# The skip term of a state space layer: a diagonal product on TensorE, or a multiply-add on VectorE

## The reference

```python
x_conv = silu(causal_conv(x_ssm) + conv_b)         # 4 taps
B_mat, C_mat = split(x_conv @ W_x + b_x)           # 16 states each
A_discrete = exp(-exp(A_log))
h = A_discrete * h + xc_t[:, :, None] * B_t[:, None, :]
y = einsum('bn,bdn->bd', C_t, h) + D_param * xc_t  # the skip term is D_param * xc_t
y = y * silu(gate)
y = y @ W_out + b_out
```

## Time and profile before

| | |
|---|---|
| median of 3 runs | 522.19 us |
| profiled execution | 522.04 us |
| its span on the core | 520.2 us |
| TensorE (PE) busy | 440.5 us, 85% |
| VectorE (DVE) busy | 395.1 us, 76% |
| GpSimd (POOL) busy | 386.6 us, 74% |
| ScalarE (ACT) busy | 290.6 us, 56% |
| chain that ended last, by engine | PE 60%, DVE 15%, ACT 10%, issue 9% |

### The profile page before, as it was taken

The page is one execution under the profiler, slowest core; times in us unless marked ns, Lnnn a source line. Parts: engine busy times, 40 slices in busy tenths (PEclk is TensorE's granted clock), DMA queues, the critical chain, the costliest instruction groups (busy, mean ns, idle before and its releaser), DMA issues.

```text
span 520.2 us, 6106 instructions
## 1 busy us (share of the span) xinstructions
PE 440.5 (85%) x1807; PEld 263.3 (51%) x1807; DVE 395.1 (76%) x683; ACT 290.6 (56%) x475; POOL 386.6 (74%) x317
## 2 busy tenths in 40 slices
PE   0784968899799989998999899989999899786653
PEld 0563844665367446754665457545655476332221
DVE  2174042885899799779997999789997979779985
ACT  2664463875467745775477647763866466433300
POOL 2554342877878988988799889977998888755583
PEclk9988797989999999999999999999999999898966
DMA  8400001721162216221633144222423152225220
GB/s 305 168 20 4 2 1 34 189 81 42 41 167 61 84 34 202 82 81 42 174 98 94 40 130 137 80 60 74 149 82 81 53 151 81 82 72 151 72 91 20
DMA packets 25379, 46.97 MB, mean 90 GB/s; under 512 B 3072, under 2 KB 4096, under 8 KB 25088
## 3 DMA queue, kind: packets, MB, share of 16 engines
q1 hardware_dynamic: 24336, 45.13, 30.2%
q10 hardware_dynamic: 1008, 1.41, 0.8%
HBM read 42.33 MB, written 4.19 MB: 89 GB/s over the span
## 4 chain that ended last, share of the span: by engine, by line
PE 60%; DVE 15%; ACT 10%; issue 9%; POOL 3%; DMA 2%; SPq 0%; DVEq 0%; ACTq 0%; POOLq 0%
PE bank0a L941 28%; PE bank1a L1021 6%; DVE hs L1371 6%; PE bank0a L1060 5%; DVE xbank L1348 4%; PE ybank L1086 3%; PE bank1a L1031 3%; PE bank1a L1006 3%; ACT xn L694 2%; PE bank0d L914 2%; DMA Bt<-w_in 1%; DVE st L1276 1%; PE ybank L1081 1%; PE bank0d L930 1%; PE bank1d L1054 1%
## 5 line engine op out<-in xcount | busy, mean ns | idle before, releaser
L556 POOL TENSOR_TENSOR hs<-hs,Ct 128x512 f32<-128x512 f32 x127 | 165.1, 1302 | 39.3 <-DVE hs L1371 24.1
L1371 DVE TENSOR_TENSOR_SCAN hs<-decay,carry,xbank 128x512 f32<-128x512 f32 x63 | 80.6, 1279 | 7.9 <-DVE xbank L1348 0.5
L1371 DVE TENSOR_TENSOR_SCAN hs<-decay,xbank 128x512 f32<-128x512 f32 x64 | 78.0, 1219 | 5.2
L518 POOL TENSOR_TENSOR hidAl<-plain,hidAh 128x512 fp32r<-128x512 f32 x48 | 66.3, 1384 | 19.2 <-ACT hidAh L653 11.9
L518 POOL TENSOR_TENSOR hidBl<-plain,hidBh 128x512 fp32r<-128x512 f32 x48 | 66.9, 1397 | 16.2 <-ACT hidBh L653 8.2
L1348 DVE TENSOR_TENSOR xbank<-xs,bbank 128x512 f32<-128x512 f32 x104 | 71.6, 689 | 7.0 <-ACT bbank L750 5.3
L652 ACT ACTIVATE plain<-bank0a,col 128x512 f32<-128x512 f32 x64 | 44.0, 687 | 39.1 <-PE bank0a L941 36.1
L941 PE MATMUL bank0a<-hidAh,hTh 128*128 128x512 f32 x128 | 55.9, 437 | 1.7 <-ACT q L685 1.7
L941 PE MATMUL bank0a<-hidBh,hTh 128*128 128x512 f32 x128 | 55.9, 437 | 1.7 <-ACT q L685 1.7
L941 PE MATMUL bank0a<-hidAl,hTh 128*128 128x512 f32 x128 | 51.9, 406 | 0.0
L941 PE MATMUL bank0a<-hidBl,hTh 128*128 128x512 f32 x128 | 51.1, 399 | 0.0
(11 more groups left out here) (190 smaller groups left out, 923.9 us busy)
## 6 DMA issues: line engine op xcount, KB each, us to landing
xs<-x_rows SPq DMA_DIRECT2D x128, 256.0 KB, 3.4
xt<-x_tok SPq DMA_DIRECT2D x8, 256.0 KB, 4.8
xr<-x_feat SPq DMA_DIRECT2D x8, 256.0 KB, 8.2
x_rows<-xc SPq DMA_DIRECT2D x8, 256.0 KB, 2.1
out<-xr SPq DMA_DIRECT2D x7, 256.0 KB, 5.4
fh<-h_w SPq DMA_DIRECT2D x1, 1024.0 KB, 9.8
hs<-h_w SPq DMA_DIRECT2D x1, 1024.0 KB, 11.6
lw<-l_w ACTq DMA_DIRECT2D x1, 640.0 KB, 5.6
```

What stands on the lines that cost most here:

```text
L518: pool.tensor_tensor(low[:, m, :], plain[:, k % NPLAIN, :], high[:, m, :].bitcast(F32), ALU.subtract).then_inc(hidden_low, 1)
L556: pool.tensor_tensor(h, h, Ct[:, hs_(u)], ALU.mult).then_inc(p_ready, 1)
L1371: dve.tensor_tensor_scan(hs[:, i % NSTATES, :], decay[:, gr:gr + 1].broadcast_to([P, HALF]), xbank[:], 0.0 if u % 2 == 0 else carry[:, k:k ...
```

## The change

The diagonal product and `d_diag` go. The first gathering product of each quarter now opens the sum (`start=(quad == 0)`). VectorE adds the skip term when it gates: one `scalar_tensor_tensor` writes xc * D + `ybank` to `yg`, a wait for its own result follows (`y_summed`), and a `tensor_tensor` multiplies `yg` by `gate` in place. In `finish_last` both sums come first, and then both products.

```diff
-            act.activation(d_diag[:], ident[:], ACT.Copy, scale=scale("D")).then_inc(d_ready, 1)
...
-                    if quad == 0:
-                        pe.wait_ge(d_ready, 1)
-                        pe.matmul(ybank[:], d_diag[:], xc[:, hs_(u)], start=True, stop=False)
...
-                                  start=False, stop=(quad == NGRP // QUAD - 1)).then_inc(y_full, 1)
+                                  start=(quad == 0), stop=(quad == NGRP // QUAD - 1)).then_inc(y_full, 1)
...
-                dve.tensor_tensor(yg[:, hs_(t)], ybank[:], gate[:, hs_(t)], ALU.mult).then_inc(yg_ready, 1)
+                dve.scalar_tensor_tensor(yg[:, hs_(t)], xc[:, hs_(t)], scale("D"), ybank[:], ALU.mult,
+                                         ALU.add).then_inc(y_summed, 1)
+                dve.wait_ge(y_summed, t + 1)
+                dve.tensor_tensor(yg[:, hs_(t)], yg[:, hs_(t)], gate[:, hs_(t)], ALU.mult).then_inc(yg_ready, 1)
...
                 for part in range(2):
-                    dve.tensor_tensor(yg[:, quarter(part)], ybank[:, half_of(part)], gate[:, quarter(part)],
+                    dve.scalar_tensor_tensor(yg[:, quarter(part)], xc[:, quarter(part)], scale("D"), ybank[:, half_of(part)],
+                                             ALU.mult, ALU.add).then_inc(y_summed, 1)
+                for part in range(2):
+                    dve.wait_ge(y_summed, t + 1 + part)
+                    dve.tensor_tensor(yg[:, quarter(part)], yg[:, quarter(part)], gate[:, quarter(part)],
                                       ALU.mult).then_inc(yg_ready, 1)
```

More of the change, by code:

```diff
@@ L209, in program @@
         b_conv = sb("b_conv", [P, 1])
-        d_diag = sb("d_diag", [P, P])
         gat = sb("gat", [P, 2 * P // QUAD - DPG])
@@ L363, in program @@
         y_full = sem("y_full")
-        d_ready = sem("d_ready")
+        y_summed = sem("y_summed")
         yg_ready = sem("yg_ready")
```

## The result

The changed kernel takes 514.47 us (median of 4 runs, 513.99 to 515.65), the kernel before 521.92 us beside it. The ratio is 0.9864, 95% interval 0.9833 to 0.9895. Two more comparisons gave 0.984 (0.979 to 0.9889) and 0.9867 (0.9838 to 0.9896). So it is faster, as forecast, but by 7.0 to 7.7 us and not by 4.6.

What follows compares the result with a forecast made beforehand. TensorE was taken to bound seven of eight units: 522.04 - 6.02 + 0 + 0.7 + 0.77 = 517.5 us, so 517.6 expected in the runs. Range 516.6 to 518.8, or 516.2 to 520.8 with the thin cover.

Steps and rivals of the forecast that it cites:

- TensorE bounds seven of eight units and the join moves by 0.86 us each time: Periods 0 to 6: losing the diagonal product brings each join on VectorE 0.86 us earlier, 6.02 us in all.
- the unmoved join: Rival: SiLU behind its table load, or GpSimd's last low part, holds the join; 523.7 us, slower; chance 0.09.
- VectorE's additions are covered: Slot 11, six joins: the longer `gate_y` fits in VectorE's idle time ahead of the join and costs nothing.
- the first kind of period: Three joins with 2.23 to about 2.5 us idle before, none in slots 11 to 15: price about 0.7 us.
- the second kind: Three joins with 2.62 us idle before and a wait in slot 12: price 1.7 us, cover at least 1.93.
- The thin cover: Rival: VectorE and GpSimd block each other whole instructions, each `gate_y` costs 1.9 us; 520.0 us; chance 0.21.
- its fourth case, VectorE as the bound: Rival: over 2.7 us for each `gate_y` before all gain is lost; at 2.7, about 522 to 523; chance 0.04.
- Period 7, +0.7: Last period, where the chain runs on VectorE through `gate_y`: 0.7 us more, between 0.7 and 1.9, all on the path.
- The end, +0.77: `finish_last`: two multiply-adds go first, so the first product starts 0.77 us later, between 0.6 and 1.0, all serial.
- the start-up at nothing: Start-up: ScalarE's making of `d_diag` is one small instruction beside TensorE's first hidden layer, so its removal gains nothing.

Runs made afterwards that it cites:

- e1: The kernel before without the diagonal product and `d_diag`, VectorE unchanged, so the skip term is missing: 513.02 us, ratio 0.9769.
- p1: The changed kernel with the `value` product in slot 14 of TensorE done twice in each of 8 periods: 524.12 us, ratio 1.0054.
- e3: The changed kernel with the diagonal product back only in the loop copy that is not run, and `d_diag` made again: 517.36 us, ratio 0.9848.
- h1: The changed kernel with the diagonal product kept on TensorE for the last unit alone, whose end is as before: 514.43 us.
- l1: The changed kernel with the diagonal product back for units 0 to 3, only in the copy not run, and `d_diag` made: 518.03 us, ratio 0.994.
- both remedies: The changed kernel with the needed loop copy placed first and the last unit's diagonal product kept on TensorE: 512.48 us, ratio 0.9835.
- e4: The kernel before with the diagonal product left out only of the loop copy that is not run: 520.24 us, ratio 0.992.
- e2: The changed kernel with the diagonal product and `d_diag` put back, so the skip term is added twice: 524.68 us, ratio 0.9978.
- e5: The changed kernel with one more product of two SBUF tensors in `gate_y` of units 0 to 5: 513.79 us, ratio 0.9833.

## Why the prediction was wrong

- **TensorE bounds seven of eight units and the join moves by 0.86 us each time:** right. 6.22 us in place of 6.02. It is TensorE's time alone (e1), and another product of that size, `value`, does the same (p1). SiLU moved along, the third GELU still waiting 0.72 us for TensorE as forecast, so the unmoved join did not occur.
- **VectorE's additions are covered:** right. The idle time ahead of the joins stayed above zero. The price in the first kind of period was 1.21 to 1.26 us, by the idle time that is missing against e1, and not 0.7, so only 0.4 us of cover were left. At the place itself it was 0.65, but the compare in slot 12 then met GpSimd (1.85 us at 267.92). It isn't fixed either: at the first of these joins four profiles with the same VectorE work in slot 11 (e3, h1, l1 and both remedies) kept 1.35 us of idle time and not 0.40. In the second kind it was 1.64 at the place (3.86 us from the sum at 314.03 to the next `times_b`, before 2.22), near the 1.7, and 1.28 to 1.39 by the idle time, so up to 1.73 us were left and not 1.4 at most. The thin cover did not decide anything. The prediction's sum for its fourth case, VectorE as the bound, is off as well: with the waits in slot 12 counted, the mean cover plus 0.86 us is about 3.0 us, not 2.7.
- **Period 7, +0.7:** right: from the sum at 470.53 to the next `times_b` at 473.09 are 2.56 us, before 1.91, so +0.65.
- **The end, +0.77:** right at 0.78, measured to the start of the projection. The other 0.52 us of that execution were the clock.
- **The step that failed** is the one that cost the start-up at nothing: "ScalarE's making of `d_diag` is one small instruction in the start-up [...]: nothing", and that the opening by four products "adds no instruction: nothing". Both are true of the instructions and false of the program. The diagonal product also stood eight times in a copy of the loop that is never run. Without it the copy that runs lies eight products nearer to the branch, and a wait of 2.10 us behind it is gone (e3, e4 show it in both directions). The row was in the chain of the kernel before, as 2.10 us of "issue" at 49.51, and I read past it, since nothing near it was edited. With those 2.1 us the sum is -6.2 + 1.4 - 2.1 = -6.9 us, against -7.0 to -7.7 in the three comparisons. The rest of the first profile's start-up, 0.85 us, lies ahead of the branch and behind the second product, near the stretches in which the kernel before had the lower clock; no run tests whether the change has a part in it. The forecast -4.6 is thus the change's own price only as the sum of its terms: the one comparison with equal start-up gave 2.95 us.

## What to carry to other kernels

Where an engine's program branches to one of two large copies, what stands in the copy that is not run can be part of the time. Look for "issue" waits right behind the branch, and put the copy that is needed first: here it was worth 5.8 us in the kernel before and 1.8 in the changed one. For an addition on a busy engine, read the idle time ahead of its next join from the row of the join, and expect the price to land one or two slots later as well, where the moved phase meets another engine. Before two traces are compared, compare the granted clock in the same stretch: at the end of this kernel it makes 0.5 us, more than the reordering of the halves.

## What the runs showed of the hardware

- **Instruction loading.** In the 16 us around the branch the queue for instructions carried three packets in both kernels of the first comparison:

```profile
q8 instruction: 3, 0.05, 1.1%
```

  With the copy placed first this row is absent there; three of those four profiles have one packet on another queue instead. That the waits are for these loads is a reading: the three packets are there in the changed kernel too, which has no wait of 2.10 us. Shown is that this wait hangs on the place of the code alone.
- **The granted clock fell behind a nearly idle stretch in some executions, and not in others.** After each join TensorE has little to do for some 4 us. At 348 to 350 us of the kernel before it was busy 0.32 of 2 us, and the clock stayed at 1.00. In e4 it was busy 0.43 of 2 us at 344 to 346 us, and the clock then fell to 1.2 GHz for the convolution that follows, in period 5:

```profile
350.00:352.00 2.00, 2.00 (x5) 1.10 (x4) 1.86 (x4) 0.19 (x1) 2.00 (x2) 0.50 0.00 0
```

  Each fall cost about 2.7 to 2.9 us (that step was 57.50 us long and not 54.6). On one chip the kernel before ran 519.55 to 528.16 us, with a mean granted clock of 0.954 in the fastest and 0.943 in the slowest execution; it has no profile there, but such falls fit, and then the ratio of e1 (0.9769) is too good. Between the first and the last join, kernels without the diagonal product showed such a fall in no profile and those with it in two (e2 and e4), but behind the last join both kinds had one (e2 and e4, and both profiles of the changed kernel with the copy first). p1 on another chip could not say whether the step's length is the cause. That stays open.
- **Two SBUF inputs.** The new product took 0.68 us beside an idle GpSimd (e5, at 263.68) and 1.46 beside one that began an instruction 0.37 us earlier, ending 0.55 us behind it. In e5 three such instructions in a row, from 263.01, took 0.73, 0.68 and 0.74 us, the first of them with 0.2 us of a GpSimd instruction left to run.
